# Low parts of a LoRA B matrix: made by GpSimd in place of VectorE, with a rounded copy from ScalarE

## The reference

```python
# x: 8 x 256 x 1024, read as 4 batches of 512 tokens in the first layer; F = 2752, rank 16
def lora_add(base, inp, A, B):
    Ab = A[layer_idx][lora_indices]
    Bb = B[layer_idx][lora_indices]
    t = jnp.einsum('bri,bni->bnr', Ab, inp)
    return base + jnp.einsum('bor,bnr->bno', Bb, t) * SCALE
gate = lora_add(jnp.einsum('bnh,fh->bnf', x, W_gate), x, A_gate, B_gate)
up = lora_add(jnp.einsum('bnh,fh->bnf', x, W_up), x, A_up, B_up)
act = jax.nn.silu(gate) * up
down = lora_add(jnp.einsum('bnf,hf->bnh', act, W_down), act, A_down, B_down)
...
x = x + _L0_cond_ref(x, ..., itok_B_2_6, 0)
x = x + _L1_cond_ref(x, ..., itok_B_1_7)     # another linear layer with bias and a scaled LoRA
```

## Time and profile before

| | |
|---|---|
| median of three runs | 1652.75 us (1651.93 to 1652.83) |
| the profiled execution | 1652.34 us, its span 1650.3 us |
| mean granted TensorE clock | 0.998 of full speed |
| busy: TensorE, VectorE, GpSimd, ScalarE | 98%, 68%, 40%, 32% of the span |
| DMA | 156 MB, mean 95 GB/s |

### The profile page before, as it was taken

One profiled execution on the slowest core, in us unless ns is written; L12 is line 12 of the kernel. 1 busy time (PEld: TensorE's weight loads), 2 busy tenths in 40 slices (PEclk: granted clock), 3 DMA queues, 4 the chain that ended last, 5 costly groups with the idle time before them and its releaser, 6 DMA issues.

```text
span 1650.3 us, 21023 instructions
## 1 busy us (share of the span) xinstructions
PE 1615.0 (98%) x7060; PEld 1314.0 (80%) x7060; DVE 1129.6 (68%) x1286; ACT 535.8 (32%) x925; POOL 653.8 (40%) x441
## 2 busy tenths in 40 slices
PE   6999999999999899999999999999999999999998
PEld 4778888888887788888888788888888887778886
DVE  5887777777768877777776665566665578856433
ACT  3744444444446444444444221111111121431110
POOL 5254444444452444444444452323332331541110
PEclk9999999999999999999999999999999999999999
DMA  8334434423433344344334742122222131013322
GB/s 158 104 91 109 144 93 106 150 80 96 120 101 91 93 105 144 98 112 146 81 80 128 275 124 67 45 77 80 80 55 77 62 70 28 18 29 80 79 52 53
DMA packets 218125, 156.12 MB, mean 95 GB/s; under 512 B 110692, under 2 KB 200164, under 8 KB 215268
## 3 DMA queue, kind: packets, MB, share of 16 engines
q1 hardware_dynamic: 169536, 114.92, 27.3%
q10 hardware_dynamic: 48356, 39.86, 7.7%
q0 software_dynamic: 128, 0.00, 0.0%
HBM read 115.38 MB, written 39.32 MB: 94 GB/s over the span
## 4 chain that ended last, share of the span: by engine, by line
PE 85%; DVE 5%; SPq 4%; issue 2%; ACT 2%; POOL 1%; DMA 1%; DVEq 0%; ACTq 0%
PE ps L1954 85%; SPq L463 1%; SPq L1207 1%; DVE X_T L614 1%; SPq L1199 1%; ACT Bf L1471 1%; SPq L1171 1%; DVE TU L514 0%; DVE TG L514 0%; POOL W L1839 0%; SPq L1224 0%; DMA raw<-in_L_cond_W_up_dram 0%; DMA act_scratch<-vbuf 0%; DVE s L547 0%; DVE s L540 0%
## 5 line engine op out<-in xcount | busy, mean ns | idle before, releaser
L1954 PE MATMUL ps<-X_T,W 128*128 128x512 f32 x1944 | 460.4, 392 | 11.8 <-DVE vbuf L683 5.2
L1954 PE MATMUL ps<-act,Wd 128*128 128x512 f32 x2016 | 462.4, 390 | 1.4 <-POOL Wd L1888 1.4
L1954 PEld LDWEIGHTS ps<-act,Wd 128*128 128x128 f32 x2016 | 378.6, 188 | 81.5 <-POOL Wd L1888 1.8
L1954 PEld LDWEIGHTS ps<-X_T,W 128*128 128x128 f32 x1944 | 364.7, 188 | 94.2 <-DVE vbuf L668 7.6
L1954 PE MATMUL ps<-X_B,W 128*128 128x512 f32 x1728 | 417.7, 392 | 14.0 <-ACT X_B L1416 13.3
L1954 PEld LDWEIGHTS ps<-X_B,W 128*128 128x128 f32 x1728 | 325.6, 189 | 83.9 <-issue 15.5
L940 DVE TENSOR_TENSOR acc<-acc,ps 128x1024 f32<-128x1024 f32 x176 | 214.1, 1220 | 176.1 <-PE ps L1954 175.6
L1839 POOL TENSOR_TENSOR W<-s,W 128x512 fp32r<-128x512 f32 x156 | 210.8, 1351 | 256.3 <-ACT W L1387 256.3
L1839 POOL TENSOR_TENSOR W<-TG,W 128x512 fp32r<-128x512 f32 x88 | 129.8, 1476 | 175.8 <-ACT W L1387 175.7
L1387 ACT ACTIVATE W<-s 128x512 fp32r<-128x512 f32 x156 | 98.4, 632 | 239.2 <-PE ps L1954 232.7
L1880 POOL TENSOR_TENSOR act<-stage,act 128x1024 fp32r<-128x1024 f32 x42 | 100.6, 2414 | 173.7 <-ACT act L1623 173.7
(11 more groups left out here) (134 smaller groups left out, 1512.2 us busy)
## 6 DMA issues: line engine op xcount, KB each, us to landing
stage<-act_scratch SPq DMA_DIRECT2D x21, 1024.0 KB, 5.0
raw<-in_L_cond_W_gate_dram SPq DMA_DIRECT2D x164, 128.0 KB, 3.0
raw<-in_L_cond_W_up_dram SPq DMA_DIRECT2D x164, 128.0 KB, 3.1
raw<-in_x_dram SPq DMA_DIRECT2D x104, 128.0 KB, 3.1
raw<-in_L_cond_W_down_dram SPq DMA_DIRECT2D x88, 128.0 KB, 3.2
act_scratch<-c21buf ACTq DMA_DIRECT2D x42, 256.0 KB, 2.4
act_scratch<-vbuf ACTq DMA_DIRECT2D x42, 256.0 KB, 2.8
xt_scratch<-xt ACTq DMA_DIRECT2D x4, 2048.0 KB, 7.0
```

Of the source, the lines that this page charges most:

```text
L1954: return nc.tensor.matmul(dst, stationary, moving, start=start, stop=stop, skip_group_check=True)
```

## The change

b_low moves from VectorE to GpSimd. For it ScalarE's `b_high` writes one instruction more at its beginning: a rounded copy of both B's, `b_round`, in the same 64 partitions as `ts`, and b_low subtracts this from `ts`. The low block of Bf now lies on the partitions of its source (block 0 for gate, block 1 for up), and the high blocks and two blocks of `Tm_u` trade places to match. The matmuls stay as they are. `b_high` waits, as the only new wait of ScalarE, for the b_low of the unit before, which reads `b_round`. On GpSimd b_low stands behind A11's low part of unit U + 1 (unit 1 of a half: behind S1's; in the first unit both behind the four low parts of unit U + 1), and it waits for the last low part made before it and, at its end, for itself.

```diff
--- before.py
+++ after.py
@@ -88,10 +88,10 @@
         tw = at("tw", 180224, [P, 2, TT])
 
         TM_HI = (slice(0, 2 * Q), slice(2 * Q, 4 * Q))
-        TM_LO = (slice(2 * Q, 3 * Q), slice(Q, 2 * Q))
-        TM_AGAIN = (slice(3 * Q, 4 * Q), slice(0, Q))
-        BF_HI = ((0, 1, 2), (1, 2, 3))
-        BF_LO = (3, 0)
+        TM_LO = (slice(2 * Q, 3 * Q), slice(0, Q))
+        TM_AGAIN = (slice(3 * Q, 4 * Q), slice(Q, 2 * Q))
+        BF_HI = ((1, 2, 3), (0, 2, 3))
+        b_round = at("b_round", 209664, [2 * Q, 256], F32R)
 
 
         acc = [at(f"acc{j}", 32768 * j, [P, KT, T]) for j in range(2)]
@@ -435,18 +435,25 @@
             wo = Wo[item[1] % 2]
             return src[:, :].rearrange("p (k m) -> p k m", k=KT)[:, ks, :], wo[:, 0, ks, :], wo[:, 1, ks, :]
 
-        def b_places(u, w, source, to, also):
-
-            src = ts[source, :].rearrange("p (r f) -> p r f", r=2)
-            homes = [Bf[u % 2][rows, w, :, :] for rows in (to, also)]
+        def b_places(u, w, source, to):
+
+            src, home = ts[source, :].rearrange("p (r f) -> p r f", r=2), Bf[u % 2][to, w, :, :]
             if u < FULL - 1:
                 src = src.rearrange("p r (q c i) -> p r q c i", q=NQ, c=2)[:, :, :, u % 2, :]
-                homes = [home.rearrange("p r (q i) -> p r q i", q=NQ) for home in homes]
+                home = home.rearrange("p r (q i) -> p r q i", q=NQ)
             elif u == FULL - 1:
                 src = src[:, :, 0:P]
             else:
-                src, homes = src[:, :, P:P + HC], [home[:, :, w * HC:(w + 1) * HC] for home in homes]
-            return src, homes[0], homes[1]
+                src, home = src[:, :, P:P + HC], home[:, :, w * HC:(w + 1) * HC]
+            return src, home
+
+        def b_rounded(u, rows):
+
+            if u < FULL - 1:
+                return b_round[rows, :].rearrange("p (r q i) -> p r q i", r=2, q=NQ)
+            if u == FULL - 1:
+                return b_round[rows, :].rearrange("p (r f) -> p r f", r=2)
+            return b_round[rows, 0:2 * HC].rearrange("p (r f) -> p r f", r=2)
 
         def load_first(eng, kind, w):
 
@@ -638,16 +645,6 @@
                             :, 0:each, :, :])
                 last.then_inc(b_turned, 1)
 
-            def b_low(U):
-                u = U % UNITS
-                eng.wait_ge(bf_hi, U + 1)
-                for w in range(2):
-                    rows = slice(w * Q, (w + 1) * Q)
-                    lo = slice(BF_LO[w] * Q, (BF_LO[w] + 1) * Q)
-                    src, dst, hi = b_places(u, w, rows, lo, rows)
-                    last = V.tensor_tensor(dst, src, hi.bitcast(F32), ALU.subtract)
-                last.then_inc(bf_lo, 1)
-
             def t_low(h, p, w):
                 cols, rows = slice(p * TT, (p + 1) * TT), slice(2 * w * Q, (2 * w + 1) * Q)
                 eng.wait_ge(t_hi, h * 4 + 2 * p + w + 1)
@@ -758,12 +755,10 @@
                 turn_tile(("U", U + 1))
                 x_low(h, "T1", 0)
                 x_sum(h, "T1", 1)
-                b_low(U)
                 x_low(h, "T2", 0)
                 for p in range(2):
                     for w in range(2):
                         t_low(h, p, w)
-                b_low(U + 1)
                 x_low(h, "T1", 1)
                 x_sum(h, "T2", 1)
 
@@ -1462,12 +1454,15 @@
                 eng.wait_ge(b_turned, U // UNITS * BLOCKS + u // 2 + 1)
                 if U >= 2:
                     wait_stage(eng, *last_stage(U - 2))
+                both = slice(0, 2 * Q)
+                if U >= 1:
+                    eng.wait_ge(bf_lo, U)
+                A.activation(b_rounded(u, both), b_places(u, 0, both, both)[0], ACT.Copy)
                 for w in range(2):
                     if u == FULL:
                         A.activation(Bf[u % 2][:, w, :, (1 - w) * HC:(2 - w) * HC], zeros[:, :, :], ACT.Copy)
                     for r in BF_HI[w]:
-                        rows = slice(r * Q, (r + 1) * Q)
-                        src, home, _ = b_places(u, w, slice(w * Q, (w + 1) * Q), rows, rows)
+                        src, home = b_places(u, w, slice(w * Q, (w + 1) * Q), slice(r * Q, (r + 1) * Q))
                         last = A.activation(home, src, ACT.Copy)
                 last.then_inc(bf_hi, 1)
 
@@ -1863,16 +1858,34 @@
                 ag_low(h, 1)
                 for item in ("A11", "A12", "A21", "A22"):
                     w_low(U + 1, item)
+                b_low(U)
+                b_low(U + 1)
 
             def second_unit(U):
-                for item in ("A11", "S2", "S1", "A12"):
-                    w_low(U + 1, item)
+                w_low(U + 1, "A11")
+                w_low(U + 1, "S2")
+                w_low(U + 1, "S1")
+                b_low(U + 1)
+                w_low(U + 1, "A12")
 
             def third_unit(U):
                 for item in ("S4", "S3", "A22"):
                     w_low(U, item)
-                for item in ("A11", "S2", "S1", "S3"):
+                w_low(U + 1, "A11")
+                b_low(U + 1)
+                for item in ("S2", "S1", "S3"):
                     w_low(U + 1, item)
+
+            def b_low(U):
+                u = U % UNITS
+                eng.wait_ge(bf_hi, U + 1)
+                eng.wait_ge(w_lo, made[0])
+                for w in range(2):
+                    rows = slice(w * Q, (w + 1) * Q)
+                    src, dst = b_places(u, w, rows, rows)
+                    last = G.tensor_tensor(dst, src, b_rounded(u, rows).bitcast(F32), ALU.subtract)
+                last.then_inc(bf_lo, 1)
+                eng.wait_ge(bf_lo, U + 1)
 
             def act_low(t, pr):
                 cols = slice(pr * T, (pr + 1) * T)
@@ -1909,12 +1922,16 @@
                 elif u < FULL - 1:
                     for item in ("A12", "A22", "S4"):
                         w_low(U, item)
-                    for item in ("A11", "S2", "S1", "S3"):
+                    w_low(U + 1, "A11")
+                    b_low(U + 1)
+                    for item in ("S2", "S1", "S3"):
                         w_low(U + 1, item)
                 elif u == FULL - 1:
                     for item in ("A12", "A22", "S4"):
                         w_low(U, item)
-                    for item in ("A11", "N", "A12", "S"):
+                    w_low(U + 1, "A11")
+                    b_low(U + 1)
+                    for item in ("N", "A12", "S"):
                         w_low(U + 1, item)
                 elif h == 0:
                     w_low(U + 1, "A11")
```

## The result

The changed kernel took 1643.6 us (median of 5 runs, 1643.09 to 1645.78) against 1652.37 us before: ratio 0.9946, 95% interval 0.9934 to 0.9958. The direction and the places were right; several terms of the sum were not.

The account below looks back on a forecast made before the run. TensorE, busy 1615 of 1650.3 us, bounds the kernel; VectorE counts only where TensorE waits, in each half's first units. Terms 2.1 + 1.5 - 0.5 + 2.2 + 1.0 = 6.3 us won: median 1646.4 us, range 1644.3 to 1650.0.

Parts of the forecast that it names:

- middle units: The 36 units of 19.9 us each, where TensorE never waits for b_low: moving it was to win nothing.
- first half, P4 of unit 2: P4 of unit 2, at 93.99 us before, was to start 2.1 us earlier, between 1.6 and 2.6.
- clock behind P4: P4's twelve matmuls in unit 2 were to lose their drop to 1.2 GHz: 1.5 us won, bounds 0 and 1.5.
- given back: Unit 3, first half: without the slow clock VectorE was to reach add_v some 0.5 us late, bounds 0 and 1.
- second half, P4 of unit 24: P4 after the second half's first units was to come 2.2 us earlier, by bounds of 2.7 and 1.7.
- b_low before unit 25: Removing b_low's 1.88 us at 549.83 was to shorten the 1.80 us wait at 565.25 by 1.0, bounds 0.5 and 1.5.
- The pair: GpSimd's two 32 x 256 subtractions per unit were to take 1.5 us, bounds 0.84 and 3.0.
- E11: TensorE's first adapter product of a unit, which needs b_low; in unit 1 it was to start at 61.7 us, before 60.48.
- The new wait: TensorE was to stand 1.2 us for GpSimd's b_low at E11 of units 1 and 23.
- Rival C: Slow matmuls behind the new gaps at 60 and 512 us cost 1.5 us each: 1649.4 us; chance 0.10.
- Rival A: The new wait eats the gain: GpSimd's pair takes 3.0 us, 1.8 us won, 1651.0 us; chance 0.12.
- Rival B: GpSimd holds VectorE up by 0.3 us in each of 36 middle units: slower, 1657 us; chance 0.05.

Follow-up runs that it names:

- first: Against the changed kernel, VectorE makes b_low for units 0 to 3 of each half from the rounded copy, GpSimd for units 4 to 21: 1654.99 us, ratio 1.0010.
- all: Against the changed kernel, VectorE makes every b_low at its old place, keeping the new layout and ScalarE's additional copy: 1654.64 us, ratio 1.0009.

## Why the prediction was wrong by a little

The result lies 0.7 us beyond the fast end of the range. What the prediction said of the places held: middle units and the end of the stage nothing, the first units of each half (up to P4 of unit 3) everything. Term by term, against the changed kernel's execution without a slow clock (before minus after, us; bounds in brackets):

```
                                        forecast           measured
start of the adapters                      -                 0.44
first half, P4 of unit 2               2.1 (1.6 to 2.6)      1.45
clock behind P4                        1.5 (0 to 1.5)        1.55
given back                            -0.5 (-1 to 0)         0.04
up to P4 of unit 9                         -                 0.51
second half, P4 of unit 24             2.2 (1.7 to 2.7)      2.74
b_low before unit 25                   1.0 (0.5 to 1.5)      1.94
behind that                                -                -0.2
sum                                    6.3                   8.5
```

*The pair, 1.5 us:* right, 1.50 to 1.52 where E11 waits for it. Beside VectorE's sums it is 2.3 to 2.4, so the bound of 3.0 had a reason. As the Trainium skill has it (GPSIMD Engine Reference, Key points), the two engines contend when VectorE reads two SBUF operands; the runs agree, with 1.51 against 2.41 us, and with 1.22 against 2.31 for VectorE.

*The new wait, 1.2 us in both halves:* 1.76 and 0.91 in the first trace, 1.77 and 0.70 in the second, 1.96 and 1.04 in the third, in sum 2.5 to 3.0 for 2.4. Near in sum, though the halves differ.

*First half, 2.1 us:* 1.45 behind the start of the adapters, too high; 1.89 with their start, which is chance (in three traces of the changed kernel the adapters began 0.44 and 0.39 us earlier than before and 0.34 later). I let VectorE's path decide; in the changed kernel VectorE waits 2.45 us for P6 (3.71 with the slow clock), so TensorE's did, and its E11 came 0.3 us later than forecast. From add_q to P4 it was 12.5 us, not 13.2 as before.

*Given back, minus 0.5:* nothing was given back. VectorE arrives at unit 3 earlier, not later: its wait for P6 there grew from 1.00 to 1.82 us.

*Second half, 2.2 us:* 2.74, just outside its bounds. From E11 to P4 the two halves win about the same (33.51 to 30.13 us and 33.72 to 30.12); E11's wait is the shorter one here.

*b_low before unit 25, 1.0 us:* this is the step that failed, with 1.94 against an upper bound of 1.5. I held back 0.3 or 0.4 us as "the usual" wait for add_v, from the earlier trace rows, and another 0.5 for sums of VectorE that GpSimd's pair might hold up. Neither cost the matmuls anything: the two sums behind add_c22 take 0.97 and 1.78 us, against 1.33 and 1.77 before. The usual waits are those of the weight loads, and a weight load's wait of 0.3 us costs the matmuls nothing. At P4 of unit 25 the weight load waited 2.22 us and the matmuls 1.80 before; after, the weight load still waits its usual 0.33, and the matmuls not at all:

```profile
565.25 2.59 PEld L1954 LDWEIGHTS ps<-X_T,W 128*128 128x128 f32 x12 [2.22 <-DVE vbuf L668]
```
```profile
558.98 2.59 PEld L1971 LDWEIGHTS ps<-X_T,W 128*128 128x128 f32 x12 [0.33 <-DVE vbuf L665]
```

The waits of both in the trace after, from 46 to 925 us (sum, times, longest), show the same: 16 waits of the weight loads for add_v, and none of the matmuls.

```profile
PE ps L1971 <- POOL Bf L1886: 2.7, 2, 1.8
PE ps L1971 <- DVE vbuf L680: 1.8, 2, 1.1
PE ps L1971 <- POOL Wd L1901: 1.5, 1, 1.5
```
```profile
PEld ps L1971 <- DVE vbuf L665: 5.4, 16, 0.5
```

The trace before had it too: of the seven waits in the earlier trace rows only the longest, 0.84 us, made the matmuls wait, for 0.42. So the 1.88 us of b_low were worth 1.9, and with VectorE making b_low of unit 3 alone the 1.80 came back.

*The clock, 1.5 us:* right where it happened, with 1.55. The prediction took it for fixed that the kernel before has the drop in its first half and the wait of 1.80 in its second. As the three traces above show them, these are alternatives that cost about the same, so the sum came out right here by luck. Rival C was right as a mechanism: the drop stood behind the new wait in two of three profiled executions of the changed kernel. Those two took 1645.78 and 1646.14 us, not 1649.4: one gap of two had the drop, not both. One drop cost 1.6 us (4.50 for 2.89), about what C gives for it; the rest of C's sum shares the terms that were priced too low.

*Up to unit 9, 0.51 us,* was in no term: 0.42 of it is that single wait of the matmuls of before for add_v of unit 9, which the prediction had said nothing of b_low reaches. It is gone with VectorE making b_low there too, so b_low isn't its cause. Ahead of that add_v VectorE itself waits 0.42 us for a load of x, and in the changed kernel it doesn't:

```profile
231.88 1.25 DVE L579 STREAM_TRANSPOSE xt<-raw 128x1024 f32<-128x1024 f32 x1 [0.42 <-DMA raw<-in_x_dram]
```

The second execution of the changed kernel has such a wait in unit 27 (0.28 us), and nothing ties either to the change: this half us is luck.

*Rival A* was tested by the doubled pair: 1649.3 us against its 1651.0 for a pair of 3.0 us. *Rival B* is out: GpSimd's doubled work costs the middle units nothing in the trace.

The range was too narrow on the fast side: its low end was 8.4 us won, about the sum of the upper bounds (8.3), one of which (1.5) was no bound. On the slow side the sum of the lower bounds is 3.8, not the 3.9 written there, which changes nothing.

## What to carry to other kernels

An instruction in an in-order queue costs its own time and the idle time in front of it, whenever work that is ready stands behind it: 0.84 us of b_low stood for some 3 us of VectorE. Price a stall by the waits of the matmuls, not by those of the weight loads, of which 0.3 to 0.4 us cost nothing here. And before a wait is shortened, look what the earlier start will lie beside: here GpSimd's pair, started 2.7 us earlier, and what followed from it won nothing and by the medians lost 2.7 us.

## What the runs showed of the hardware

One kernel, one wait, two clocks: behind waits of 1.76, 1.96, 2.04 and 2.84 us at 62 us the granted clock fell to 0.50 for some 3 us, behind waits of 1.77, 1.90 and 2.44 us at the same place it stayed at 1.00 (2.4 GHz). Before P4 of unit 2 it was the same: of the waits of 2.57 to 2.62 us in the traces of before, first and all, three had a fall behind them and three had not. The length of the wait alone doesn't decide here, and one profile can't say which it will be.

A 32 x 256 subtraction on GpSimd took 0.73 to 0.75 us beside VectorE's transposes and up to 1.62 beside its sums of two SBUF operands; VectorE's 128 x 1024 subtraction went from 1.22 to 1.65 us beside such a pair and to 2.31 beside a 128 x 512 low part, while its transposes of 128 x 1024 kept to 1.20 to 1.25 us.
